# Edge attributes turned in the neighbour stage and kept in a scratch table for the attention stage

## The reference, cut to what matters

```python
gathered = embeddings[edge_col] * edge_val[:, None]                     # layer 0: the neighbour stage
relevant = segment_sum(gathered, edge_row, num_segments=N)
x = layernorm(x + relevant @ W1 + (relevant * x) @ W2)
q, k, v = x @ Wq + bq, x @ Wk + bk, x @ Wv + bv                         # layer 1: attention over edges
e = edge_attr @ We + be                                                 # (E, 64) @ (64, 128)
logits = ((q[dst] * k[src]).sum(-1) + (q[dst] * e).sum(-1)) * SCALE     # for each head
attn = softmax of logits over the edges of one dst
out = segment_sum(attn[..., None] * v[src], dst) @ Wo + bo
x = layernorm(x + out)
```

## Time and profile before

| what | value |
|---|---|
| median of 3 runs | 13507.12 us |
| the profiled execution: its time / its span | 13492.22 us / 13490.6 us |
| mean granted TensorE clock of that execution | 0.727 of full speed |
| neighbour stage, first to last scatter | about 230 to 6215 us of the span |
| attention stage, first to last weight copy | 6671.5 to 13195.4 us of the span |
| HBM traffic | 1271 MB read, 286 MB written |

### The profile page before, as it was taken

The page is one execution under the profiler, slowest core; times in us unless marked ns, Lnnn a source line. Parts: engine busy times, 40 slices in busy tenths (PEclk is TensorE's granted clock), DMA queues, the critical chain, the costliest instruction groups (busy, mean ns, idle before and its releaser), DMA issues. The chain is left out here.

```text
span 13490.6 us, 212064 instructions
## 1 busy us (share of the span) xinstructions
PE 7773.5 (58%) x49074; PEld 6032.7 (45%) x49074; DVE 5368.0 (40%) x19840; ACT 3708.5 (27%) x8489; POOL 8166.4 (61%) x6569
## 2 busy tenths in 40 slices
PE   2444444444444444445577777777777777777774
PEld 1433433343343333343355555555555555555552
DVE  3333333333333333334444444444444444444447
ACT  1111111111111111111144444444444444444441
POOL 2888888888888888884344444444444444444440
PEclk6666666666666666666777787777778777777786
DMA  8666666666666666665444444444444444444441
GB/s 195 105 105 107 106 106 105 107 105 105 106 106 106 105 107 106 105 107 141 129 121 122 123 122 122 122 121 122 121 121 124 120 122 121 121 123 122 120 122 44
DMA packets 2212139, 1558.78 MB, mean 116 GB/s; under 512 B 734904, under 2 KB 1995514, under 8 KB 2211832
## 3 DMA queue, kind: packets, MB, share of 16 engines
q0 software_dynamic: 628992, 668.10, 29.2%
q1 hardware_dynamic: 1519265, 835.24, 22.1%
q10 hardware_dynamic: 63832, 54.86, 1.4%
HBM read 1271.07 MB, written 286.16 MB: 115 GB/s over the span
## 5 line engine op out<-in xcount | busy, mean ns | idle before, releaser
L506 POOL DMA_INDIRECT rel_sum<-sums,row x3224 | 5003.5, 1552 | 1209.8 <-issue 624.0
L1087 POOL DMA_INDIRECT kv<-kv_rows,src_idx x3232 | 3084.2, 954 | 3493.3 <-DVE msg L1317 2566.9
L462 PE MATMUL coef_ps<-same,spread 128*128 128x128 f32 x6448 | 1634.6, 437 | 3572.7 <-DVE spread L435 2952.0
L462 PEld LDWEIGHTS coef_ps<-same,spread 128*128 128x128 f32 x6448 | 1423.2, 325 | 3749.9 <-DVE spread L435 3116.8
L1335 DVE TENSOR_TENSOR acc<-acc,out_ps 128x256 f32 x3232 | 1363.1, 422 | 1978.6 <-remote 889.5
L449 DVE TENSOR_TENSOR row<-moved,src_col 128x8 int32<-128x8 f32 x403 | 69.2, 172 | 3782.9 <-DMA rel_sum<-sums,row 3782.8
L1130 PE MATMUL ring_ps<-pick,q_win 128*128 128x128 f32 x6464 | 1259.5, 356 | 245.8 <-ACT pick L1420 186.9
L1130 PEld LDWEIGHTS ring_ps<-pick,q_win 128*128 128x128 f32 x6464 | 1101.9, 257 | 653.1 <-issue 648.9
L490 ACT ACTIVATE sums<-sum_ps 128x512 f32<-128x512 f32 x806 | 437.6, 595 | 2884.4 <-DMA rel_sum<-sums,row 2882.1
L435 DVE TENSOR_SCALAR spread<-iota_n,rel_col,w_col 128x128 f32<-128x128 f32 x3224 | 1213.1, 381 | 0.0
L431 DVE SCALAR_TENSOR_TENSOR same<-src_bc,src_col,later 128x128 f32<-128x128 f32 x3224 | 1114.2, 346 | 180.7 <-issue 118.5
(11 more groups left out here) (177 smaller groups left out, 7339.7 us busy)
## 6 DMA issues: line engine op xcount, KB each, us to landing
q_win<-q_rows SPq DMA_DIRECT2D x3232, 64.0 KB
src_bc<-src_flat SPq DMA_DIRECT2D x403, 512.0 KB
x_win<-in_x SPq DMA_DIRECT2D x3224, 64.0 KB
attr<-in_edge_attr SPq DMA_DIRECT2D x804, 128.0 KB
mark<-marks ACTq DMA_DIRECT2D x202, 256.0 KB
kv<-kv_rows,src_idx POOLq DMA_INDIRECT x3232
rel_sum<-sums,row POOLq DMA_INDIRECT x3224
rep<-rel_sum SPq DMA_DIRECT2D x100, 256.0 KB, 3.8
```

Source lines behind the costliest of these rows:

```text
L462: last = nc.tensor.matmul(coef_ps[k][:, i, :], spread[:, b, j, :], same[:, b, j, :], start=True, stop=True)
L506: pool.indirect_dma_start(out=rel_sum[r], out_offset=bass.IndirectOffsetOnAxis(ap=row[:, b, j:j + 1], axis=0), in_=sums[:, b, j, :], in_of ...
L1087: pool.indirect_dma_start(out=kv[:, 2 * i + u, k * S + s, :], out_offset=None, in_=kv_rows, in_offset=bass.IndirectOffsetOnAxis(ap=src_idx ...
```

## The change

The neighbour stage loads the attributes of its own 1,024 edges (256 KB, one run of 2 KB a partition), turns them on PE with 8 transposes into two PSUM banks of their own (64 partitions), lets ACT copy them out in the order of the edges, and stores 64 rows of 4 KB to a new table in HBM, `attr_cols`. The attention stage loads `attr_t` from this table, now double-buffered, with features on partitions (runs of 512 bytes), and `attr_fill`, `attr_drain`, their semaphores and two of the ten places of `PERIOD` are gone. In `prepare` some semaphores are merged.

```diff
@@ neighbours: SP's body @@
+                    wait_alone(sp, attr_filled, 2 * (s.g - 1), passed)
...
+                        sp.dma_start(attr[:, b, :, :], edge_attr[bass.ds(s.g * GP, GP), :].rearrange(
+                            "(p j) f -> p j f", j=G)).then_inc(attr_in[b], 16)
                     wait_alone(sp, sum_done, 2 * (s.g - 1), passed)
                     start = load_starts(sp, regs, start_row[0:1, bass.ds(s.g * G, G)], LAST)
                     for j in range(G):
                         sp.dma_start(x_win[:, b, j, :], x[bass.ds(start[j], P), :]).then_inc(x_in[b], 16)
 
+                    keep_attr(s.plus(-1))
+
+                def keep_attr(s):
...
+                    wait_alone(sp, attr_turned, 2 * s.g + 2, passed)
+                    sp.dma_start(attr_cols[:, bass.ds(s.g * GP, GP)], turned[:, b, :]).then_inc(attr_kept[b], 16)
@@ neighbours: PE's body, between the matmuls of L462 and of L471 @@
+                    wait_alone(pe, attr_in[b], s.uses(2) * 16 + 16 * (isinstance(s.u, int) and s.g == NG - 1), passed)
+                    for k in range(2):
+                        wait_alone(pe, attr_turned, s.g * 2 - 1 + k, passed)
+                        for j in range(4):
+                            last = nc.tensor.transpose(attr_ps[k][:, j, :], attr[:, b, k * 4 + j, :], ident[:])
+                        last.then_inc(attr_filled, 1)
                     pe.wait_ge(x_in[b], s.uses(2) * 16 * G)
@@ neighbours: ACT's body, between L484 and L486 @@
+                    if not isinstance(s.u, int) or s.g >= 2:
+                        act.wait_ge(attr_kept[b], s.plus(-2).uses(2) * 16)
+                    for k in range(2):
+                        act.wait_ge(attr_filled, s.g * 2 + k + 1)
+                        nc.scalar.activation(turned[:, b, :].rearrange("f (p k j) -> f k j p", k=2, j=4)[:, k],
+                                             attr_ps[k][:], ACT.Copy).then_inc(attr_turned, 1)
@@ attention @@
-PERIOD = (("q", 1, 2), ("q", 1, 3), ("pick", 2, 0), ("pick", 2, 1), ("attr", 2, 0), ("q", 2, 0), ("pick", 2, 2),
-          ("q", 2, 1), ("attr", 2, 1), ("pick", 2, 3))
+PERIOD = (("q", 1, 2), ("q", 1, 3), ("pick", 2, 0), ("pick", 2, 1), ("q", 2, 0), ("pick", 2, 2),
+          ("q", 2, 1), ("pick", 2, 3))
...
-        attr = sb("attr", [P, 2, S, 2, ED])
-        attr_t = sb("attr_t", [P, S, P])
+        attr_t = sb("attr_t", [P, 2, S, P])
...
                 def load_attr(n, u):
-                    wait_alone(sp, attr_filled[u], n.plus(-1).count(), passed)
+                    wait_alone(sp, ke_done[2 * u + 1], n.plus(-1).count(), passed)
                     if n.is_under(NG - 1):
-                        rows = edge_attr[bass.ds(n.g * AP, AP), :].rearrange("(s q p) f -> q p s f", q=B, p=P)
+                        tiles = attr_cols[:, bass.ds(n.g * AP, AP)].rearrange("f (s q p) -> q f s p", q=B, p=P)
                         for h in range(2):
-                            sp.dma_start(attr[:, u, :, h, :], rows[2 * u + h]).then_inc(attr_in[u], 16)
+                            sp.dma_start(attr_t[h * ED:(h + 1) * ED, u, :, :], tiles[2 * u + h]).then_inc(attr_in[u], 16)
...
                     pe.wait_ge(kv_in[slot], n.landed(16 * U))
-                    pe.wait_ge(attr_drained[u], n.count())
+                    attr_landed(n, u)
...
-                        attr_fill(m, 0)
...
-                        attr_fill(m, 1)
...
-                        attr_drain(m, 0)
...
-                        attr_drain(m, 1)
```

More of the change, by code:

```diff
@@ L195, in prepare @@
         psum = [ctx.enter_context(nc.psum_tensor(f"turn{i}", [P, 512], F32)) for i in range(2)]
[L196 to L199, removed]
+        filled, loaded, padded, prep_stored = (sem(n) for n in (
+            "filled", "loaded", "padded", "prep_stored"))
+        iota_done, const_done, vec, turned, copied = (sem(n) for n in (
+            "iota_done", "const_done", "vec", "turned", "copied"))
         with nc.Block() as block:
@@ L390, in neighbours @@
         coef = sb("coef", [P, 2, G, P])
+        attr = sb("attr", [P, 2, G, ED])
+        turned = sb("turned", [ED, 2, GP])
         sums = sb("sums", [P, 2, G, D])
@@ L393, in neighbours @@
         sum_ps = [ctx.enter_context(nc.psum_tensor(f"sum_ps{i}", [P, 4, P], F32)) for i in range(2)]
+        attr_ps = [ctx.enter_context(nc.psum_tensor(f"attr_ps{i}", [ED, 4, P], F32)) for i in range(2)]
+        attr_in, attr_kept = ([sem(f"{n}{i}") for i in range(2)] for n in ("attr_in", "attr_kept"))
+        attr_filled, attr_turned = sem("attr_filled"), sem("attr_turned")
+        LEFT = (E - (NG - 1) * GP) // G
+        SPARE = E - (NG - 1) * GP - LEFT * G
+        assert 0 < LEFT and 0 < SPARE < G
         starts_in, src_in, x_in = sem("starts_in"), [sem(f"src_in{i}") for i in range(2)], [sem(f"x_in{i}") for i in range(2)]
@@ L415, in body @@
                         sp.dma_start(x_win[:, b, j, :], x[bass.ds(start[j], P), :]).then_inc(x_in[b], 16)
+                    keep_attr(s.plus(-1))
+                def keep_attr(s):
+                    if isinstance(s.u, int) and s.g < 0:
+                        return
+                    b = s.turn(2)
+                    wait_alone(sp, attr_turned, 2 * s.g + 2, passed)
+                    sp.dma_start(attr_cols[:, bass.ds(s.g * GP, GP)], turned[:, b, :]).then_inc(attr_kept[b], 16)
                 steps(sp, NG, 2, 2, 1, body)
+                keep_attr(Step(0, NG - 1, 2))
+                for b in range(2):
+                    sp.wait_ge(attr_kept[b], (NG + 1 - b) // 2 * 16)
             @block.vector
@@ L1100, in bank_free, with attr_landed @@
                     elif then.is_from(0):
[L1101 removed]
+                        pe.wait_ge(q_drained[at], then.count())
                     return ring_ps[place_of(kind, k)[0] % 2]
[L1104 removed]
+                def attr_landed(n, u):
                     full = n.is_under(NG - 1)
@@ L1110, in attr_fill @@
                         pe.wait_ge(attr_in[u], n.count(32, 32 - 16 * loads))
-                    to = bank_free("attr", n, u)
-                    for s in range(S):
-                        mm = nc.tensor.transpose(to[:, s, :], attr[:, u, s, :, :].rearrange("p h f -> p (h f)"), ident[:])
-                    mm.then_inc(attr_filled[u], 1)
                 def pick_fill(n, k):
@@ L1145, in keys @@
                         nc.tensor.matmul(ke_ps[k][:].rearrange("p s e -> p (s e)"), we[half, :],
-                                         attr_t[half, :, :].rearrange("p s e -> p (s e)"), start=False, stop=True
+                                         attr_t[half, u, :, :].rearrange("p s e -> p (s e)"), start=False, stop=True
                                          ).then_inc(ke_done[2 * u + k], 1)
@@ L1226, in body @@
                         out_bank(c, 3)
-                    if new:
-                        attr_fill(m, 1)
                     if mid:
@@ L1239, in _ @@
                 body(Group(0, -1))
-                groups(pe, NG, HEAD, TAIL, {1: range(6), 2: range(1, 11), 32: range(96, 161, 32),
+                groups(pe, NG, HEAD, TAIL, {1: range(6), 2: range(1, 11), 32: range(64, 161, 32),
                                             16 * U: range(32 * U, 80 * U + 1, 16 * U)}, ((16 * U, 1), (16 * U, 2), (16, 1), (16, 2)), body)
```

36 lines of the change are left out of this document (17 added, 19 removed).

## The result

The change makes the kernel slower: 13656.73 us (median of 4 runs, 13645.33 to 13662.21) against 13505.46 us for the kernel before beside it, ratio 1.0111, 95% interval 1.0098 to 1.0125. That is 151 us more, where 13220 us was forecast.

What follows compares the result with a forecast made beforehand. It took POOL's scatter issue to bound the neighbour stage and a chain through PE with two stalls a group to bound attention. 13492 - 283 = 13209 us, plus 15 us for the runs' median, gave about 13220 us, range 12880 to 13420.

Steps and rivals of the forecast that it cites:

- Neighbour stage, landing: Neighbour-stage scatters: behind the added 0.52 MB, landing goes from 2.4 to 4.1 us, under the 5.87 us margin; cost 0.
- Rival C: Neighbour stage: scatters land later than 5.87 us and POOL waits at L505; 500 us more, net 13720 us; chance 8%.
- Neighbour stage, SP's order: SP's list: the store waits for the turned copy, the next source load goes some 4 us later; cost 0.
- Neighbour stage, PE and ACT: 8 transposes (2.5 us at most) and two 0.6 us copies a step, covered by an 11.6 us margin; cost 0.
- Attention, 1.4 us a group: Attention stage: removed transposes and copies save 0.7 + 0.5 + 0.2 us a group, 283 us in all.
- The 0.7 us for the first transposes: Attention, PE: the first four removed transposes stand on the chain just before the logits; saves 0.7 us a group.
- The 0.5 us for the exponent: Attention, ACT: the second removed copy stood straight ahead of the exponent; saves 0.5 us a group.
- the 0.2 us for the ring: Attention: `q_fill(m, 0)` waits for an earlier `pick` copy, PE starts up to 0.7 us sooner; a quarter counted.
- Rival B: Attention: gain swallowed by a PE clock falling from 0.79 to 0.74, or stalls ending at a fixed moment; about 13490 us; 14%.
- Rival A: Attention: PE's stalls shrink too, by some 1.5 us a group, another 300 us; about 12920 us; chance 15%.
- The sum: Whole kernel: neighbour stage 0, attention -283 us, giving 13209 us, forecast as 13220 us with the runs' 15 us offset.

Runs made afterwards that it cites:

- n_late: Kernel before with only the change's neighbour stage, the store kept in SP's queue but issued one step later so it never waits: 13500.87 us, ratio 0.9997.
- n_actstore: Kernel before with only the change's neighbour stage, the store issued from ACT's queue right behind its copies: 13515.0 us, ratio 1.0010.
- n_nodma: Kernel before with only the neighbour stage's transposes and copies, without the attribute load and the store: 13498.26 us, ratio 0.9995.
- p_late: Changed kernel with the store issued one step later so SP never waits: ratio 0.9987 to the kernel before, which took 13708 us there.
- a_half: Kernel before with 8 of the 16 key and value gathers a group, in bursts of 4 in place of 8: 11747.36 us in one run.
- a_drain: Kernel before, POOL waiting inside a group until the last four gathers have landed before issuing four more: ratio 1.1276, kernel before 11044.66 us.
- a_drain2: Same kernel as a_drain on another chip, where the kernel before took 11052 us: ratio 1.1302.
- a_drain3: Same kernel as a_drain on a third chip, where the kernel before took 11047 us: ratio 1.1272.
- a_pace: Kernel before with a group's 16 gathers released in four lots of 4 by events of groups in work: 13166.54 us, ratio 0.9749.
- a_pace2: Same kernel as a_pace on another chip, where the kernel before took 11044.66 us: ratio 1.0001.

## Why the prediction was wrong

**Neighbour stage, landing: failed.** The step reads "If a scatter has to stand behind the whole of it ... landing goes from 2.4 to 4.1 us, still under 5.87". It counted only the added 0.52 MB. What a scatter meets is all that is on the way at once: store, sources, attributes and windows, 1.5 MB. At the prediction's 302 GB/s that would have been 5 us on top, over the margin; the landings read were 5.1 us in the timeline and 6.0 us or more in the slowest twentieth of the steps. Rival C named the place (L505's wait), the price per scatter and the deciding point, 5.87 us, rightly; it was given 8% and 500 us, for landings of 6.5 us throughout. Only some steps passed the point: 226 of 3,224 scatters started clearly late (over 2.0 us), for 150 us in all.

**Neighbour stage, SP's order: failed.** "the source load of the next step, which so is issued some 4 us later; it is wanted a step and more later" is right as to when the load is wanted: no wait of DVE for it shows from 2000 to 4000 us. SP's wait was 7.6 us and not 4, and the step did not ask what the delayed load would run into. n_late and n_actstore, which take this one wait out of SP's list, take the whole loss back.

**Neighbour stage, PE and ACT: right.** Cost 0, as n_nodma shows, though a copy took 1.12 us in place of 0.6; the cover was wide enough.

**Attention, 1.4 us a group: failed.** The gain came out as 0, also with the neighbour stage mended (p_late). The prediction set the stalls aside as something that the change doesn't touch, and then counted work as if they moved with it. Its three terms failed in two ways. The 0.7 us for the first transposes stood ahead of a release that comes some 1.9 us after the burst, in both kernels: a chain that ends in such a wait gives back whatever is cut ahead of it. The earlier trace rows already showed ACT and DVE idle with all they waited for long done; the rows that were not read were POOL's beside them. The 0.5 us for the exponent and the 0.2 us for the ring stood behind the release, where DVE's list (sums 2.08 us, then messages) and not ACT's led to POOL's next burst. Both did come sooner, by some 0.4 and 0.7 us, but the messages did not.

Rival B had the first of these in one sentence ("It also ends there if the stalls last until a fixed moment"), at 14% together with the clock. The clock did fall, to 0.77 and not to 0.74: PE's busy time fell by 84 us, where 202 x 1.47 = 297 us of transposes went. The rule of the Trainium skill (TensorE: Matmul & The Clock Gate, "HAM oscillation") that idle stretches between bursts of matmuls put the clock back agrees with the fall to 0.77. That the lower clock is not what swallowed the gain is argued, not shown: behind the release DVE ran without waiting for PE. With the clock full and no late release, on the other chips, the period did not hang on PE either. Rival A, stalls that shrink, did not occur.

**The sum.** Forecast 0 for neighbours and -283 us for attention; measured +150 and 0. B's attention and a part of C's neighbour stage came together, a case that the text did not have.

## What to carry to other kernels

Before a DMA that waits is put into a queue, look at what stands behind it: held back, those loads leave in one burst with the next ones, and transfers of another queue with little margin land late, while the mean DMA share doesn't show it. Issue such a store one step late, so that it doesn't wait. And where an idle engine resumes long after its producer is done, find what ends that wait before counting any saving ahead of it, and behind it follow the engine whose instructions have no gap. The period may belong to an engine that is busy half of the time.

## What was not expected of the hardware

- On the chips where the kernel before took 13506 to 13708 us, ACT and DVE waited up to 8 us for releases of TensorE while POOL issued indirect gathers back to back (0.95 us each, 1.25 us apart), though TensorE's instructions were done some 6 us before. The last such wait ended about 1.9 us after the last gather of eight, and about 1.1 us after the last of four in a_half. On three other chips (a_drain, a_drain2 and a_drain3 each met another) there was no such wait, with the same program, and it took 11045 to 11052 us. The neighbour stage's scatters were 1.857 us apart in both cases.
- The same pacing edit (a_pace, a_pace2) gave 0.9749 on one chip and 1.0001 on another, so a gain in this stage has to be measured on both.
- A ScalarE copy of 64x512 float32 out of PSUM took 1.12 us, with an output whose elements are 8 apart, against 0.60 us for 128x512 written in one run.
